# Attention and feed-forward layer on one core: f16 output projection, narrower band product, no loop over the pairs, new engine orders

## The reference

```python
x = x + layernorm(attention(layernorm(x)))       # x: 8 batches x 1024 tokens x 256, f32
x = x + layernorm(ffn(layernorm(x)))
# attention: 16 heads of 64
q, k, v = x @ Wq[h], x @ Wk[h], x @ Wv[h]
scores = q @ k.T / 8 + bias[h, clip(s - t + 16)] # relative bias, causal mask
out = (softmax(scores) @ v, heads side by side) @ Wp + bp      # 1024 -> 256
# ffn
xr, xk = mu * x + (1 - mu) * x_prev              # x_prev: x one token earlier
out = sigmoid(xr @ W_r) * (relu(xk @ W_k) ** 2 @ W_v)
```

## Time and profile before

| | us |
|---|---|
| median of 3 runs | 2397.01 (2396.01 to 2399.61) |
| the profiled execution's own time | 2398.64 |
| its span, first to last instruction | 2396.8 |
| PE, DVE, ACT, POOL busy | 2260.2, 1971.8, 1662.1, 1496.9 |

### The profile page before, as it was taken

The page is one execution under the profiler, slowest core; times in us unless marked ns, Lnnn a source line. Parts: engine busy times, 40 slices in busy tenths (PEclk is TensorE's granted clock), DMA queues, the critical chain, the costliest instruction groups (busy, mean ns, idle before and its releaser), DMA issues.

```text
span 2396.8 us, 80999 instructions
## 1 busy us (share of the span) xinstructions
PE 2260.2 (94%) x29568; PEld 1542.8 (64%) x29568; DVE 1971.8 (82%) x3848; ACT 1662.1 (69%) x2524; POOL 1496.9 (62%) x2593
## 2 busy tenths in 40 slices
PE   3788889999999999999999999999999999999986
PEld 1355556667666666666766766666676676667675
DVE  6688888888888888788888888788888888888846
ACT  2577777777777777677776777677777777777743
POOL 2244345777767777677776777677777766566752
PEclk9899999999999999999999999999999999999998
DMA  6011111122112112212111221121221221121230
GB/s 166 27 40 42 37 52 48 47 63 68 62 52 68 53 42 69 62 51 68 53 56 55 62 66 53 54 63 47 69 61 54 65 63 51 40 63 57 63 109 21
DMA packets 182461, 140.42 MB, mean 59 GB/s; under 512 B 10400, under 2 KB 173088, under 8 KB 182048
## 3 DMA queue, kind: packets, MB, share of 16 engines
q1 hardware_dynamic: 182048, 134.98, 18.7%
HBM read 57.81 MB, written 43.06 MB: 42 GB/s over the span
## 4 chain that ended last, share of the span: by engine, by line
PE 88%; DVE 5%; issue 3%; DMA 2%; ACT 1%; POOL 1%; SPq 0%; POOLq 0%; DVEq 0%; ACTq 0%
PE score_ps L607 16%; PE misc L563 14%; PE misc L690 8%; PE misc L578 7%; PE misc L671 6%; PE misc L672 6%; PE misc L673 6%; PE max_ps L629 5%; PE score_ps L611 5%; PE max_ps L637 2%; PE misc L715 2%; PE misc L683 2%; PE misc L704 2%; PE misc L707 2%; DVE row_max L1209 1%
## 5 line engine op out<-in xcount | busy, mean ns | idle before, releaser
L1576 POOL TENSOR_TENSOR probs<-probs_f,probs 128x1024 f16<-128x1024 f32 (+1 forms) x320 | 617.3, 1937 | 215.6 <-ACT probs L970 215.5
L1209 DVE TENSOR_REDUCE row_max<-max_ps 128x2 f32<-128x1024 f32 (+2 forms) x640 | 632.7, 1006 | 107.5 <-PE max_ps L637 106.7
L952 ACT ACTIVATE probs_f<-score_ps,score_unit 128x1024 f32<-128x1024 f32 (+1 forms) x320 | 331.0, 1034 | 226.7 <-DVE score_ps L1225 189.3
L671 PE MATMUL misc<-v_pair,probs 128*128 128x65 f16 x4608 | 436.3, 193 | 6.4 <-DVE q_lo L1168 4.3
L672 PE MATMUL misc<-v_pair,probs 128*128 128x64 f16 x4608 | 436.0, 193 | 0.0
L673 PE MATMUL misc<-v_pair,probs 128*128 128x65 f16 x4608 | 435.4, 193 | 0.0
L1193 DVE TENSOR_TENSOR probs<-score_ps,probs 128x1024 f16<-128x1024 f32 (+3 forms) x448 | 373.6, 836 | 73.6 <-ACT probs L970 55.8
L671 PEld LDWEIGHTS misc<-v_pair,probs 128*128 128x128 f16 x4608 | 417.0, 97 | 19.7 <-issue 11.7
L672 PEld LDWEIGHTS misc<-v_pair,probs 128*128 128x128 f16 x4608 | 417.4, 97 | 7.0
L673 PEld LDWEIGHTS misc<-v_pair,probs 128*128 128x128 f16 x4608 | 417.5, 97 | 0.1
L952 ACT ACTIVATE score_ps<-score_ps,score_unit 128x1024 f32<-128x1024 f32 (+3 forms) x448 | 351.9, 786 | 93.3 <-DVE score_ps L1225 87.7
(11 more groups left out here) (166 smaller groups left out, 4058.6 us busy)
## 6 DMA issues: line engine op xcount, KB each, us to landing
v_pair<-v_calc SPq DMA_DIRECT2D x64, 516.0 KB, 3.8
o_scratch<-o_stage SPq DMA_DIRECT2D x128, 256.0 KB, 2.5
o_cur<-o_scratch SPq DMA_DIRECT2D x56, 512.0 KB, 4.0
xh<-x SPq DMA_DIRECT2D x56, 128.0 KB, 2.2
x_res<-x SPq DMA_DIRECT2D x56, 128.0 KB, 2.3
out<-out_sb SPq DMA_DIRECT2D x56, 128.0 KB, 1.7
shift_all<-shift_row SPq DMA_DIRECT2D x256, 1.0 KB
probs<-wqkv SPq DMA_DIRECT2D x1, 3072.0 KB, 13.3
```

Of the source, the lines that this page charges most:

```text
L671: pe.matmul(bank[:, at:at + D + 1], high, v_high, start=j == 0, stop=False)
L952: nc.scalar.activation(dst, score_ps[t % 2][:, :, 0:width], ACT.Exp, scale=score_unit[:]).then_inc(exp_done, 1)
L1209: last = dve.tensor_reduce(dst[:, :, i % 4:i % 4 + 1], max_ps[:, :, col:col + width], AX.X, ALU.max)
L1576: pool.tensor_tensor(low, copy_of(par + ahead, t)[:, 0:2 * width], high, ALU.subtract).then_inc(lo_done_pool, 1)
```

## The change

1. **Output projection in f16.** `wp` is scaled by a power of two and split into high and low f16 parts on the chip (its maximum is found in unit 2, reduced over the partitions by POOL in unit 3, scales made in unit 4, high part by ACT in unit 5, low part by DVE in unit 6). ACT's copy of the transposed outputs writes the f16 high part, DVE subtracts it for the low part (`outputs_low`, twice a unit), and the projection is 24 f16 matmuls of 256 columns where it was 8 f32 ones (16 instructions). `projected` multiplies by a unit before it adds `bp`. The tail does the same. The scaling of `wp` ahead of the first unit goes.
2. **Band.** The half `r = 1` comes first and has 80 columns where it had 144 (128 in the first block).
3. **No loop.** All 66 bodies are written out.
4. **Orders.** New `TASKS`, and new orders on PE, ACT, DVE, POOL (low part of tile 4 ahead of `residual_norm`) and SP (the store of o2 and o3 goes to the end of the body, `load_head` ahead of `load_shift`). In the tail ACT does `last_outputs` 5 to 7 ahead of norms.

PE's new order in a full unit: ffn, fill 0, score 1, o2, q0, q1, fill 1, score 2, score 3, o0, o3, ot0, score 4, fill 2, o1, ot1, fill 3, score 5, score 6, k0, mt0, k1, fill 4, score 7, score 8, fill 5, v0, fill 6, score 9, x2t, proj, fill 7, score 10, xt, v1, fill 8, rk, score 11, score 0 of the next unit, mt1. ACT's: exponential and high part of each tile 1 to 11 in turn (q0, q1 after tile 1; ot0 after 3; ot1 after tile 4; shift 0, k0 after 5; k1 between the two steps of 6; v0 between those of 7; xt, v1 late), gate, tile 11, shift 1, tile 0 of the next unit.

```diff
-TASKS = [("q0", 1, "qkv"), ("ffn", 0, "ffn"), ("o2", 1, "prev"), ("ot0", 0, "proj"), ("o0", 1, "att"),
...
+TASKS = [("ffn", 0, "ffn"), ("o2", 1, "prev"), ("q0", 0, "qkv"), ("q1", 1, "qkv"), ("o0", 0, "att"),
+         ("o3", 1, "prev"), ("ot0", 0, "proj"), ("o1", 1, "att"), ("ot1", 0, "proj"), ("k0", 1, "qkv"),
+         ("k1", 0, "qkv"), ("v0", 1, "qkv"), ("x2t", 0, "mix"), ("proj", 1, "proj"), ("xt", 1, "xt"),
+         ("v1", 0, "qkv"), ("rk", 1, "mix")]
...
-SPANS = [(n, n + 1) for n in range(-2, 10)] + [(10, 50)] + [(n, n + 1) for n in range(50, N)]
+SPANS = [(n, n + 1) for n in range(-LEAD, N)]
...
-                        for r in range(2):
+                        for r, part in ((1, WIN - D), (0, window)):
                             for h in range(2):
                                 rows = slice(D * h, D * h + D)
-                                last = pe.matmul(max_ps[:, h, col + width - window:col + width], half_ident[rows, r, :],
-                                                 band_bf[rows, (at + 1) % NPAIR, r, WIN - window:WIN],
-                                                 start=False, stop=r == 1)
+                                last = pe.matmul(max_ps[:, h, col + width - part:col + width], half_ident[rows, r, :],
+                                                 band_bf[rows, (at + 1) % NPAIR, r, WIN - part:WIN],
+                                                 start=False, stop=r == 0)
...
+            def project_outputs(bank, parts):
+                for c in range(H * D // P):
+                    for step, (a, w) in enumerate(((0, 0), (0, 1), (1, 0))):
+                        last = pe.matmul(bank[:, 0:C], parts[:, a, c, :], wp_split[:, w, c, :],
+                                         start=c == 0 and step == 0, stop=c == H * D // P - 1 and step == 2)
+                return last
...
-                pe.wait_ge(oT_ready, 2 * (n - PROJ_LAG + 1))
+                pe.wait_ge(oT_lo_ready, 2 * (n - PROJ_LAG + 1))
                 bank = opened("proj", n, span)
-                for c in range(H * D // P):
-                    last = pe.matmul(bank[:, 0:C], oT[:, c, :], wp_sb[:, c, :], start=c == 0, stop=c == H * D // P - 1)
-                last.then_inc(full["proj"], 1)
+                project_outputs(bank, oT).then_inc(full["proj"], 1)
...
+            def outputs_low(name, n):
+                half = int(name[2])
+                dve.wait_ge(oT_ready, 2 * (n - PROJ_LAG) + half + 1)
+                cols = slice(half * 4, half * 4 + 4)
+                dve.tensor_tensor(oT[:, 1, cols, :], misc[BANK[name]][:].rearrange("p (c t) -> p c t", c=4),
+                                  oT[:, 0, cols, :], ALU.subtract).then_inc(oT_lo_ready, 1)
...
-                dve.tensor_tensor(y[:], misc[BANK["proj"]][:, 0:C], bp_sb[:], ALU.add).then_inc(y_ready, 1)
+                dve.scalar_tensor_tensor(y[:], misc[BANK["proj"]][:, 0:C], proj_unit[:], bp_sb[:], ALU.mult,
+                                         ALU.add).then_inc(y_ready, 1)
...
+            def find_wp_top():
+                for k in range(2):
+                    last = dve.tensor_reduce(wp_top[:, k:k + 1], wp_f32[k], AX.XY, ALU.max, apply_absolute_value=True)
+                last.then_inc(wp_top_ready, 1)
...
+            def split_wp():
+                for k in range(2):
+                    dve.wait_ge(wp_hi, k + 1)
+                    dve.scalar_tensor_tensor(wp_split[:, 1, 4 * k:4 * k + 4, :], wp_f32[k], wp_scale[:],
+                                             wp_split[:, 0, 4 * k:4 * k + 4, :], ALU.mult,
+                                             ALU.subtract).then_inc(wp_ready, 1)
...
-                dve.wait_ge(small_in, 16 * 7)
-                dve.tensor_scalar(wp_sb[:], wp_sb[:], pow2[:, 2:3], 1.0 / W_TOP, ALU.mult,
-                                  ALU.mult).then_inc(vec_setup, 1)
+                dve.wait_ge(small_in, 16 * 8)
                 dve.tensor_scalar(wv_sb[:], wv_sb[:], 0.5, None, ALU.mult).then_inc(vec_setup, 1)
...
+            last_outputs_low(0)
+            last_outputs_low(1)
             for j in range(2):
                 last_projected(j)
+                last_outputs_low(j + 2)
             last_projected(2)
+            last_outputs_low(4)
             mix(N)
             last_projected(3)
+            last_outputs_low(5)
             last_scales(0, 0, 0)
             last_projected(4)
+            last_outputs_low(6)
...
             last_projected(5)
             last_scales(1, 0, 1)
+            last_outputs_low(7)
```

More of the change, by code:

```diff
@@ L726, in body @@
                     ring = (m + LEAD // 2) // (NPAIR // 2) % 2 * T
-                    if has["qkv"]:
-                        project_qk("q0", n, pair * P, ring, span)
-                    if has["att"]:
-                        score(m, par, 0, 1, at)
+                    if has["ffn"]:
+                        tail_value(n, span)
                     if has["next"]:
@@ L736, in body @@
                     if has["att"]:
-                        score(m, par, 0, 2, at)
-                    if has["ffn"]:
-                        tail_value(n, span)
+                        score(m, par, 0, 1, at)
                     if has["prev"]:
                         weigh_values(2, m, par, 1, span)
-                    if has["proj"]:
-                        tail_transpose("ot0", n, span)
-                    if has["att"]:
-                        score(m, par, 0, 3, at)
+                    if has["qkv"]:
+                        project_qk("q0", n, pair * P, ring, span)
+                        project_qk("q1", n, pair * P, ring, span)
                     if has["next"]:
@@ L764, in body @@
                     if has["att"]:
+                        score(m, par, 0, 5, at)
                         score(m, par, 0, 6, at)
                     if has["qkv"]:
-                        project_v("v0", n, 4 * par, pair // 2 * 2 * P, ring, span)
+                        project_qk("k0", n, pair * P, ring, span)
                     if has["next"]:
@@ L778, in body @@
                         fill(m, par, 5, at)
+                    if has["qkv"]:
+                        project_v("v0", n, 4 * par, pair // 2 * 2 * P, ring, span)
+                    if has["next"]:
+                        fill(m, par, 6, at)
+                    if has["att"]:
+                        score(m, par, 0, 9, at)
                     if has["mix"]:
                         tail_residual_transpose(n, span)
-                    if has["att"]:
-                        weigh_values(1, m, par, 0, span)
-                        score(m, par, 0, 9, at)
-                    if has["next"]:
-                        fill(m, par, 6, at)
                     if has["proj"]:
@@ L799, in body @@
                         score(m, par, 1, 0, at)
-                        fill(m, par, 8, at)
-                    if has["xt"]:
-                        head_transpose(n, span)
-                    if has["mix"]:
-                        tail_gate_and_key(n, span)
-                    if has["next"]:
                         transpose_maxima(1, n)
@@ L1457, in body @@
                         head_low(n + HEAD_LEAD, col, misc[BANK["xt"]])
+                    if has["att"]:
+                        add_bias(m, par, 0, 10, at)
+                        low_probs(m, par, 0, 9)
+                    if has["next"]:
+                        maxima(m, par, 1, 8)
+                    if has["qkv"]:
+                        values_low("v1", m, par)
+                    if has["att"]:
+                        add_bias(m, par, 0, 11, at)
                     if has["next"]:
@@ L1461, in body @@
                         statistics("y", y, n - PROJ_LAG, y_ready, n - PROJ_LAG + 1)
+                    if has["next"]:
+                        add_bias(m, par, 1, 0, at)
                     if has["att"]:
```

251 lines of the change are left out of this document (154 added, 97 removed).

## The result

| | us |
|---|---|
| before, median of 4 runs | 2398.3 (2396.0 to 2399.6) |
| after, median of 4 runs | 2431.0 (2428.7 to 2433.9) |
| ratio | 1.0138, 95% interval 1.0121 to 1.0156 |
| predicted | 2315 (2290 to 2354) |

The change makes the kernel slower by 1.4%, where I had forecast 3.4% faster. It lies outside the range and on the other side of before, and my rival on that side (B, POOL holds o2) is not what happened.

The account below looks back on a forecast made before the run. PE was taken to bound full units. Savings of loop 22.2 + 4.0, full units 45.4 + 1.8, early 8 - 5, start 1, tail 5 sum to 82.4 us: from 2397.0 to 2315, range 2290 to 2354.

Parts of the forecast that it names:

- B: Rival, 6%: PE sits at o2 in every unit, waiting for POOL's tile 8; at 2 us a unit 2423 us.
- loop: Units of the loop: written out, pauses (22.2 us) and slightly longer units (4.0 us) go; bounds 0 and 26.2.
- projection, a full unit: On PE: 24 f16 matmuls take 2.62 us where f32 took 3.65, saving 1.03 us a unit.
- order on PE, a full unit: PE: changes from 64-row to 128-row products cost about 0.09 us each; 9 instead of 8, so +0.09 us.
- SP costed at 0: SP's queue: the moved store of o2 and o3 and `load_head` have microseconds of slack, cost 0; without slack some 2 us.
- units 0 to 7, with the split: Early units: new order gives about 31.1 us each, 8 us less; splitting `wp` on DVE adds 5 us.
- unit 63 and tail: End of kernel: 0.9 us less in unit 63, 5 us less in the f16 tail (tail bounds 0 and 7).
- the places with little slack: Fill 6, proj, xt, mt1, score 1, ffn: under 0.3 us to spare, charged 0.20 us a unit together, bounds 0 and 1.03.
- A: Rival, 18%: DVE at 31.5 of 33.64 us waits so often that full units stay at 34.7 us; 2360 us.
- C: Rival, 6%: the straight program pauses for instructions, 22.2 us coming back once in eight units; 2337 us.
- E: Rival, 2%: the projection's weight loads are not hidden on PE, each projection costing 4.97 us; 2461 us.
- D: Rival, 8%: orders better than thought, full units at 33.5 us and early ones at 30.4; 2291 us.

Follow-up runs that it names:

- run 5: Kernel before with only the loop over units 10 to 49 written out: 2369.9 us, ratio 0.9877.
- run 10: run 7 with the output projection in f32 as before, no split of the weights, no low parts of the outputs: 2388.2 us, ratio 0.9967.
- run 11: run 7 with the band's second product back at its old width of 144 columns: 2353.4 us, ratio 0.9814.
- runs 3 and 4: Kernel before plus one unread 8-column DVE maximum ahead of the maxima of fill 8: two SBUF operands 2482.3 us, one-operand reduction 2399.9 us.
- Run 6: Changed kernel with the one-operand join and SP's queue back in the order of the kernel before: 2398.8 us, ratio 1.0001.
- run 1: Changed kernel with the join of the maxima as a one-operand reduction at the same place: 2399.5 us, ratio 1.0001.
- Run 13: run 7 with rk directly behind v1, ahead of fill 8 on PE, and v1's low part ahead of fill 8's maxima on DVE: 2370.3 us, ratio 0.9881.
- run 7: Changed kernel with the one-operand join and an SP order with head first and nothing waiting behind POOL: 2342.8 us, ratio 0.9762.

## Why the prediction was wrong

| term | predicted, us | measured, us | from |
|---|---|---|---|
| loop | -26.2 | -28.4 | run 5 |
| projection, a full unit | -1.03 | -0.91 | run 10 |
| band, a full unit | -0.10 | -0.17 | run 11 |
| order on PE, a full unit | +0.09 | +0.46 | 34.06 - (34.68 - 0.91 - 0.17) |
| waits, a full unit: the join | part of +0.20 | +1.44 | 35.50 - 34.06 |
| waits, a full unit: the burst | SP costed at 0 | +0.18 | 1855.6 / 52 - 35.50 |
| a full unit | 33.84 | 35.68 | 1855.6 / 52 |
| up to the first unit | -1 | -1.6 | two runs that start alike differ by as much (81.8 in before, 80.0 in run 5) |
| units 0 to 7, with the split | -3 | +3.6 | |
| units 8 and 9 | -1.7 | +0.2 | |
| unit 62 | -0.9 | +1.5 | |
| unit 63 and tail | -5.9 | +3.7 | |

**The step that failed** is the one under DVE, where the places with little slack are charged 0.20 us together. mt1 after the joined maxima was among the six, and it is the only one of the six that waits in full units, 1.44 us a unit where the six together had 0.20. I asked of each place only whether its producer is late in its own queue, with the duration that it had before. The join's duration was not its own: it depends on what POOL does at that moment. The trace of before had it: the same 8 columns took from 152 to 774 ns, and the earlier trace rows show POOL's 3.24 us stretch, in which the join stood at 1434.14, 0.2 us before the first tile's end (the line is shown under runs 3 and 4). In 51 of the 53 units from 10 on the join of before, too, ended within 0.03 us of tile 8. The new order starts it 0.33 us behind the start of that tile in place of 1.94 us. The Trainium skill has this rule (SBUF — State Buffer, Who interferes with whom): a DVE instruction with two SBUF inputs contends with a GpSimd (here POOL) instruction that reads SBUF, whoever issues first keeps the shared pair for its whole instruction and the other blocks, and `tensor_reduce` on this chip never contends. The traces agree: 1.5 to 2.1 us with two SBUF operands in full units, 0.16 with one, at the same moment. The other order, in which DVE issues first and POOL waits, no run here shows. I cited another rule of the skill in the prediction and did not hold this one against DVE's list of operations, in which the join is the only one of a unit with both inputs in SBUF.

**The second step that failed** is the sentence on SP, "both have slack of microseconds, cost 0". I looked at what each moved DMA needs and who needs it. I did not look at what stands ahead of it: the store of o2 and o3 was moved behind `store_out`, which waits for POOL up to the end of the unit, so a slack of most of a unit was gone at once, and it came into the same 3 us as the values, the outputs and the head. And I counted the head's slack up to xt on PE, but DVE's queue stops for it at its statistics, which the new order takes 1.8 us earlier in the unit. Run 6 shows that this is enough: with SP's moves undone the loss is the same. In the changed kernel the join's wait hid most of this, 0.18 us a unit; without the join's wait it is 57 us. The price that I gave for the case without slack, "some 2 us", is of the size of the single waits of DVE for the head in run 1 (0.7 to 3.2 us).

**PE's own work** was right in its large terms (0.12 us too much for the projection, 0.07 too little for the band) and wrong in the order's: +0.46, not +0.09. I counted the changes from 64 to 128 rows and took one price for all. The steps show that the price depends on what stands on both sides: x2t took 0.28 us behind a band product of fill 5 in the old order and takes 0.47 behind the shift of score 9, rk with its start 1.95 against 1.76. That such changes make up all of the 0.46 is not shown: it is what is left when runs 10 and 11 are taken off. Run 13 takes one such change out and PE's work falls by 0.22 us.

**Early units.** The wait of 1.8 us at fill 7 is there as worked out (1.81), and one of 0.65 us for a low part, for my 0.6. Not foreseen were 0.87 at mt1 and 0.83 at the fill that waits for the row of shifts. At full clock such a unit takes 31.7 us for my 31.1, and it doesn't always have that clock (below). The runs also part the two terms of the -3. Run 10 has the new orders without the split of `wp`: its units 0 to 7 take 258.2 us, run 7 takes 265.0 with the split and run 5 takes 258.7 with the old orders. So the split cost 6.8 us for my +5, and the orders brought 0.5 us for my 8, what the clock took included in both.

**Tail.** From unit 63 on PE's work fell by 3.7 us, but DVE's rose from 64.7 to 76.6, and PE once waits 4.9 us for a low part. Below that stretch of before, then of after. The mean clock fell too, from 0.90 to 0.87. The bound of 0 that I gave the gain was not low enough. Run 10, with an f32 tail, takes 127.9 us from there on, run 7 takes 129.3: the f16 form with its low parts and its new order on ACT, -5 in the sum, loses 1.4 us here.
```profile
2271.30:2396.80 125.50, 96.23 (x861) 79.15 (x860) 64.65 (x231) 54.33 (x108) 49.57 (x95) 0.90 0.20 66
```
```profile
2300.00:2430.00 130.00, 92.54 (x933) 75.92 (x933) 76.60 (x251) 56.10 (x108) 49.99 (x95) 0.87 0.19 65
```

**Rivals.** A is the nearest: waits ate the projection, but not because DVE was full (32.7 of 35.5 us, of which 1.7 is the join's own waiting), and it stopped at 2360 because I let waits take back no more than the projection brings. B did not occur: no wait at o2 in full units. C did not: PE waits for issue nowhere between 400 and 2200 us in after. E did not: in after the 24 matmuls take 2.71 us by the next start, not 4.97, with their 98 ns loads hidden, so the rule behind it in the Trainium skill (TensorE: Matmul & The Clock Gate, the section on packing small matmuls) does not hold for these loads. D did not occur: full units are at 34.06 us even without both losses, not 33.5.
```profile
1473.03 0.44 PE L725 MATMUL misc<-ident,y 128*128 128x128 f32 x2
1473.50 2.78 PE L712 MATMUL misc<-wp_split,oT 128*128 128x256 f16 x24
1476.21 0.39 PE L651 MATMUL max_ps<-k_hi,q_hi 64*128 64x512 f16 x2
```

**What stays open**: why the full unit of the old orders with the one-operand join (34.32 us) keeps 0.3 us more than PE's terms and its two waits make, how much of the early units' length is theirs and how much the clock's, and which of the tail's waits takes the f16 form's gain.

## What to carry to other kernels

When an order is changed, an operation's old duration is only good if what ran beside it is still the same: look at the spread of a line (152 to 774 ns here) before you copy its mean, and ask of each DVE operation with both inputs in SBUF what POOL does at that moment. A transfer that is moved on a queue takes over the waits of all that now stands ahead of it, and one that is not moved comes too late when its reader is moved forward: count its slack up to the first instruction that stops for it. Two losses that lie in the same units cover each other, so undo them together before you judge either.

Both cures together, with nothing else of the change touched, give 2342.8 us: 2.4% faster than before, 3.6% faster than the change as it was made, and within the wide range that I had given for it, though not within the forecast's own 2302 to 2332. That is partly luck: the range was that wide for D, C and half of A, and not for PE's order and projection, the early units and the tail, which keep 2342.8 above 2315.

## What the hardware showed

- A DVE operation on 8 columns waits up to 2.1 us for a POOL instruction that it has no data in common with, if both of its inputs lie in SBUF, and ends 0.02 us behind it. As a reduction of one input it does not wait (0.16 us), and neither does a `tensor_tensor` with one input in SBUF and one in PSUM (0.42 us). The wait counts as busy time of DVE in the profile.
- PE's clock after short waits. In run 7 the early units have nearly the same waits (1.8, 0.9 and 0.8 us), and take 31.7 us at a granted clock of 1.00 or 34.0 at 0.90, a mean over time at both levels, 1.2 and 2.4 GHz:
```profile
147.30:181.30 34.00, 30.43 (x421) 0.90 0.20 56
215.30:247.00 31.70, 27.53 (x420) 1.00 0.21 60
```
In before, with no wait over 1.4 us there, an early unit has 1.00. In the even unit shown under run 1, a wait of 2.39 us is followed by a stretch at the lower level (0.68, then 0.50, from 1206 to 1210 us), so that 2.7 us of waiting make the unit 4.4 us longer.
- The pauses of the loop were worth what they looked: 28.4 us (interval 25.4 to 33.3) for 26.2. The 40 units written out show no wait of PE for issue.
